# A post-norm block's feed-forward residual: added token by token on GpSimd and VectorE in place of TensorE products with the identity, and the second normalisation in fused steps

## What is computed

```python
x1 = layernorm(r1) * ln1_g + ln1_b
ff = maximum(x1 @ W1 + b1, 0) @ W2 + b2        # 128 -> 512 -> 128
y  = layernorm(x1 + ff) * ln2_g + ln2_b
x3 = layernorm(x + y)                           # x: the block's input, no gain
```

## Time and profile before

| | |
|---|---|
| median of 3 runs | 623.52 us (620.82 to 624.37) |
| the profiled execution | 623.5 us |
| its span, first to last instruction | 621.7 us |
| mean granted TensorE clock | 0.97 |
| instructions | 42741 |

### The profile page before, as it was taken

The page is one execution under the profiler, slowest core; times in us unless marked ns, Lnnn a source line. Parts: engine busy times, 40 slices in busy tenths (PEclk is TensorE's granted clock), DMA queues, the critical chain, the costliest instruction groups (busy, mean ns, idle before and its releaser), DMA issues.

```text
span 621.7 us, 42741 instructions
## 1 busy us (share of the span) xinstructions
PE 518.8 (83%) x18003; PEld 442.0 (71%) x18003; DVE 520.0 (84%) x1761; ACT 440.1 (71%) x877; POOL 405.1 (65%) x523
## 2 busy tenths in 40 slices
PE   0269999999999789998565798898889888898886
PEld 0148888888888566777534688787777777787775
DVE  5547898989899377786478799999999999999982
ACT  3336776767777537776327589988898888988892
POOL 8425537555552235364127789988998888988992
PEclk9989999999999899999678799999999999999999
DMA  6875985755545200100001323332333223332232
GB/s 202 263 230 179 275 249 173 207 162 175 160 129 184 92 17 23 30 17 1 9 10 39 75 52 82 84 74 61 80 80 84 68 63 84 80 80 68 68 79 49
DMA packets 45198, 64.33 MB, mean 103 GB/s; under 512 B 5488, under 2 KB 37360, under 8 KB 42608
## 3 DMA queue, kind: packets, MB, share of 16 engines
q1 hardware_dynamic: 45168, 63.97, 37.1%
HBM read 36.29 MB, written 8.65 MB: 72 GB/s over the span
## 4 chain that ended last, share of the span: by engine, by line
PE 37%; DVE 35%; issue 14%; POOL 5%; DMA 3%; SPq 2%; ACT 2%; DVEq 1%; POOLq 0%; ACTq 0%
PE ps L758 7%; DVE top L1409 7%; DVE hid L1458 6%; DVE prod L1467 5%; PE ps L817 5%; DVE r_x L1452 4%; PE ps L738 4%; PE ps L830 4%; PE ps L773 4%; DVE best L1420 4%; PE ps L748 3%; PE ps L784 2%; PE ps L923 2%; DMA prod<-terms 2%; SPq L403 1%
## 5 line engine op out<-in xcount | busy, mean ns | idle before, releaser
L972 ACT ACTIVATE arena<-ps 128x512 f32<-128x512 f32 x128 | 69.8, 595 | 54.9 <-PE ps L758 54.7
L923 PE MATMUL ps<-arena,hid 128*32 128x32 f32 x8192 | 78.8, 199 | 30.8 <-DVE hid L1458 26.6
L923 PEld LDWEIGHTS ps<-arena,hid 128*32 128x32 f32 x8192 | 75.3, 111 | 36.4 <-DVE hid L1458 14.3
L1200 DVE TENSOR_REDUCE row_max<-ps 128x8 f32<-128x768 f32 x64 | 61.0, 953 | 20.7 <-PE ps L748 20.4
L932 PEld LDWEIGHTS ps<-xT,downT_sb 128*128 128x128 f32 x528 | 66.7, 198 | 12.6 <-issue 11.7
L758 PE MATMUL ps<-ident,arena 128*128 128x128 f32 x512 | 69.6, 281 | 0.0
L944 PE MATMUL ps<-up_sb,prod 128*128 128x128 f32 x528 | 67.7, 282 | 0.3 <-DVE prod L1467 0.3
L932 PE MATMUL ps<-xT,downT_sb 128*128 (+1 forms) x528 | 66.6, 281 | 0.0
L738 PE MATMUL ps<-tile_rows 100*32 100x96 bf16 x2112 | 36.7, 214 | 35.7 <-POOL tile_rows L563 24.9
L1203 DVE TENSOR_TENSOR arena<-ps,row_max 128x768 f32<-128x768 f32 x64 | 61.3, 958 | 5.2 <-DVE row_max L1200 2.2
L672 POOL TENSOR_TENSOR wq_sb<-wq_sb,tile_rows 128x1024 f32<-128x1024 f32 x32 | 65.1, 2034 | 0.7 <-POOL tile_rows L666 0.6
(11 more groups left out here) (164 smaller groups left out, 1359.1 us busy)
## 6 DMA issues: line engine op xcount, KB each, us to landing
arena<-r_x SPq DMA_DIRECT2D x128, 128.0 KB, 2.4
early<-terms SPq DMA_DIRECT2D x8, 720.0 KB
xT<-terms SPq DMA_DIRECT2D x8, 720.0 KB
hid<-terms SPq DMA_DIRECT2D x8, 720.0 KB
prod<-terms SPq DMA_DIRECT2D x8, 720.0 KB
x_pair<-in_x_wrapped SPq DMA_DIRECT2D x16, 256.0 KB, 4.1
xT_tile<-xT SPq DMA_DIRECT2D x34, 64.0 KB, 1.9
x<-in_x SPq DMA_DIRECT2D x8, 256.0 KB, 2.8
```

The costliest lines, as they stand in the source:

```text
L923: mm = nc.tensor.matmul(slots[32 * g:32 * g + 32, k, c], leftT[p][:, r // 2, r % 2, :], blocks_of[p][:, :, r // 2, r % 2, GROUP * g:GROUP ...
L972: return nc.scalar.activation(out_ap, in_ap, ACT.Copy)
L1200: V.tensor_reduce(mx.rearrange("p (a b) -> p a b", a=2), sc, AX_X, ALU.max).then_inc(max_done, 1)
```

## The change

The residual no longer goes through TensorE. GpSimd makes `x1_b2` = y1 * ln1_g + (ln1_b + b2) token by token, in two 128x512 instructions (`x1_and_b2`), for batch 0 at the end of the attention stage and for batch n + 1 behind the second root of batch n, ahead of `x_and_bias`. VectorE adds it to the output products in `ln2_stats`, into `r2` in SBUF, and takes the statistics from there. The second normalisation becomes two bursts of four 128x128 scalar_tensor_tensor: `ln2_centre`, (r2 - mean) * ln2_g, in place in r2, ahead of the wait for the roots, and `ln2_apply`, r2 * rstd + x_lnb. ScalarE's second eviction and TensorE's eight identity products go. The gain ln1_g and the sum ln1_b + b2 are now held as 128x128 rows, so there are ten early weights in place of eight, the last pair after SP's pair of tiles 9.

```diff
@@ buffers
-        b2_col = sb("b2_col", [P, 1])
-        out_bias = sb("out_bias", [P, 1])
+        ln1_g_all = sb("ln1_g_all", [P, P])
+        x1_bias_all = sb("x1_bias_all", [P, P])
-        x1T_b2 = tile_rows[:, 512:1024]
+        x1_b2 = tile_rows[:, 512:1024].rearrange("p (a d) -> p a d", a=4)
@@ SP
-        N_WEIGHTS = 8
+        N_WEIGHTS = 10
-                    (ln2_b_all[:], row(ln2_b)), (b2_col[:], col(b2)),
+                    (ln2_b_all[:], row(ln2_b)), (scratch[:], row(b2)),
+                    (ln1_g_all[:], row(ln1_g)), (x1_bias_all[:], row(ln1_b)),
-                    for dst, src in itertools.islice(weights, 0 if i >= 9 else 2):
+                    for dst, src in itertools.islice(weights, 0 if i >= 10 else 2):
@@ GpSimd
+            def x1_and_b2(n, q):
+
+                pool.wait_ge(y1_done, n + 1)
+                need(pool, residual_added, n)
+                hold(pool)
+                nc.gpsimd.tensor_tensor(x1_b2, y1[q], bcast(ln1_g_all[:], 1, 4), ALU.mult).then_inc(x1_step, 1)
+                pool.wait_ge(x1_step, n + 1)
+                hold(pool)
+                nc.gpsimd.tensor_tensor(x1_b2, x1_b2, bcast(x1_bias_all[:], 1, 4), ALU.add).then_inc(x1_b2_ready, 1)
+
             rsqrt(0, 1, 3)
             x_and_bias(0, 0, 0)
             pool.wait_ge(pv_done, GROUPS * NT)
+            pool.wait_ge(bias_summed, 1)
+            x1_and_b2(0, 0)
...
                     rsqrt(2 * n + 2, 0, 1)
                     if not (last and q == 1):
+                        x1_and_b2(n + 1, 1 - q)
                         x_and_bias(n + 1, i + q, 1 - q)
@@ TensorE
             def y1_transpose(n, q):
                 pe.wait_ge(y1_done, n + 1)
-                need(pe, x1T_b2_done, n)
+                need(pe, x1T_copied, n)
...
             def output_products(n, q):
 
-                pe.wait_ge(x1T_b2_done, n + 1)
-                need(pe, r2_normed, n - 1)
-                for a in range(4):
-                    nc.tensor.matmul(ps[:, 3 + 3 * q, a * P:(a + 1) * P], x1T_b2[:, a * P:(a + 1) * P], ident[:],
-                                     start=(a == 0), stop=False, skip_group_check=True)
+                need(pe, residual_added, n - 1)
                 pe.wait_ge(relu_done, FC * (n + 1))
                 for a in range(4):
                     for c in range(FC):
                         mm = nc.tensor.matmul(ps[:, 3 + 3 * q, a * P:(a + 1) * P], hidT[:, c, a * P:(a + 1) * P],
-                                              w2_sb[:, c, :], start=False, stop=(c == FC - 1), skip_group_check=True)
+                                              w2_sb[:, c, :], start=(a == 0 and c == 0), stop=(c == FC - 1),
+                                              skip_group_check=True)
@@ ScalarE
-                nc.scalar.activation(x1T_b2[:], ps[:, 0, :], ACT.Identity, bias=out_bias[:], scale=ln1_g_col[:]
-                                     ).then_inc(x1T_b2_done, 1)
...
-            a.wait_ge(bias_summed, 1)
             hidden(0)
@@ VectorE
             def ln1_apply(n, q, place=1):
                 need(v, x1T_done, n - 1)
+                need(v, x1_b2_ready, n - 1)
                 ln_apply(place, r1[q], y1[q], y1_done)
 
             def ln2_stats(n, q):
                 v.wait_ge(ff2_done, n + 1)
-                return ln_stats(0, ps[:, 3 + 3 * q, :].rearrange("p (a d) -> p a d", a=4))
+                v.wait_ge(x1_b2_ready, n + 1)
+                V.tensor_tensor(r2, ps[:, 3 + 3 * q, :].rearrange("p (a d) -> p a d", a=4), x1_b2, ALU.add
+                                ).then_inc(residual_added, 1)
+                v.wait_ge(residual_added, n + 1)
+                return ln_stats(0, r2)
+
+            def ln2_centre(n, q):
+
+                for a in range(4):
+                    last = V.scalar_tensor_tensor(r2[:, a, :], r2[:, a, :], moments[:, a, 0:1], ln2_g_all[:],
+                                                  ALU.subtract, ALU.mult)
+                last.then_inc(r2_normed, 1)
 
             def ln2_apply(n, q):
-
-                ln_apply(0, ps[:, 3 + 3 * q, :].rearrange("p (a d) -> p a d", a=4), r2, r2_normed)
                 v.wait_ge(r2_normed, n + 1)
-                V.tensor_tensor(r2, r2, bcast(ln2_g_all[:], 1, 4), ALU.mult).then_inc(r2_scaled, 1)
-                v.wait_ge(r2_scaled, n + 1)
                 v.wait_ge(xlnb_ready, n + 1)
                 need(v, x3_done, n)
-                V.tensor_tensor(r3, r2, x_lnb[q][:], ALU.add).then_inc(r3_done, 1)
+
+                for a in range(4):
+                    last = V.scalar_tensor_tensor(r3[:, a, :], r2[:, a, :], rstd[:, a:a + 1], x_lnb[q][:, a, :],
+                                                  ALU.mult, ALU.add)
+                last.then_inc(r3_done, 1)
...
-                    V.tensor_tensor(out_bias[:], ln1_b_col[:], b2_col[:], ALU.add).then_inc(bias_summed, 1)
+                    V.tensor_tensor(x1_bias_all[:], x1_bias_all[:], scratch[:], ALU.add).then_inc(bias_summed, 1)
...
                     ln2_stats(n, q).then_inc(stat_step, 1)
                     ln_moments(2 * n + 2, 0, 1)
+                    ln2_centre(n, q)
                     v.wait_ge(rstd_done, 2 * n + 2)
```

More of the change, by code:

```diff
@@ L269, in attention_and_product_keys @@
         bias_summed = sem("bias_summed")
-        x1T_b2_done = sem("x1T_b2_done")
+        x1_step = sem("x1_step")
+        x1_b2_ready = sem("x1_b2_ready")
+        residual_added = sem("residual_added")
         x1T_done = sem("x1T_done")
@@ L281, in attention_and_product_keys @@
         r2_normed = sem("r2_normed")
-        r2_scaled = sem("r2_scaled")
         r3_done = sem("r3_done")
```

## The result

The changed kernel takes 631.08 us (median of 4 runs, 630.01 to 631.94), the kernel before 622.63 us beside it (620.82 to 624.37): ratio 1.012, 95% interval 1.0094 to 1.0147. It is slower by about 8.5 us; 12.5 were forecast. One execution in all that follows (675.38 us at a mean granted TensorE clock of 0.753, of the kernel with the fused steps alone) was in a slower state of the chip and is left out of its median.

The account below looks back on a forecast made before the run. TensorE was taken to bound the feed-forward before the change, GpSimd's row after it. Through batch 5 +12.2 us, batch 6 +0.35, batch 7 about nothing: +12.5 on 623.5 gave 636.0 us, range 625 to 641.

Parts of the forecast that it names:

- The mechanism: Feed-forward: VectorE's SBUF-to-SBUF steps stand still beside GpSimd's 128x512 instructions; batch 12.4 us in place of 10.25.
- TensorE's gain: Feed-forward batch: without eight identity products, output products wait for the last ReLU; 0.28 us gained, loop 9.97 us.
- VectorE's own costs: VectorE alone, per batch: added addition 0.69 us, each fused burst of four 1.11; round in 8.3 us.
- Root done at +6.3: Steady batch, counted from its start at 260.44: GpSimd's second reciprocal root ends 6.3 us in.
- Three of the seven slip in, four follow: VectorE's seven steps left after the root: three pass during GpSimd's row, four follow it, taking 1.1 us.
- Some 5.0 with three insertions: GpSimd's row behind the second root holds the port 4.76 us, some 5.0 with three VectorE steps inserted.
- Costed at nothing: Attention stage: one more pair of weight loads, 1.3 us once if uncovered; bias sum at most 0.28 once; both taken as 0.
- two steps per boundary: Rival in the feed-forward: two VectorE steps pass per GpSimd boundary, about 631 us; two or three together had chance 0.25.
- No lock: Rival: VectorE's new bursts are not held beside GpSimd, TensorE stays the bound; -2.9 us, about 620.6; chance 0.12.
- shut out: Rival: VectorE's seven steps all wait for the last of GpSimd's row; about 640 us; chance 0.15.
- The signs named beforehand: Feed-forward: batches 12 to 12.7 us apart, TensorE about 80% busy waiting for ln1_apply, held VectorE steps about 1.2 us each.
- one step per boundary: Main case: one VectorE step passes between two GpSimd instructions; batch 12.4 us, total 636; chance 0.45.

Follow-up runs that it names:

- the kernel with the fused steps alone: Kernel before with only the second normalisation as two bursts of four fused steps, residual still through TensorE: median 623.12 us, ratio 0.9983.
- The pair moved: Changed kernel with GpSimd's two new instructions of a batch put behind the zero fill and VectorE's last burst: median 625.33 us, ratio 1.0042 to the kernel before.
- left out: Changed kernel without GpSimd's two new instructions in batches 1 to 7: median 621.35 us, ratio 0.9965 to the kernel before.
- cut up: Changed kernel with each of GpSimd's two new 128x512 instructions cut into four of 128x128, same place: median 622.34 us, ratio 0.9991 to the kernel before.
- The kernel with the loads: Kernel before with later tiles placed as in the changed kernel and two more weights loaded, ten in all: 622.85 us, ratio 0.999.

## Why the prediction was right, and where its size was off

- **The mechanism** was right: VectorE's steps from SBUF behind the second root stand still beside GpSimd's 128x512 instructions, one passes per boundary, and GpSimd's row becomes the pace. The pair moved, left out and cut up each took the cost away.
- **TensorE's gain** of 0.28 us a batch: the batch was 9.88 to 9.97 where VectorE was free. Right.
- **VectorE's own costs**: addition 0.69, burst 1.14 (1.11 taken). Right. By the estimate from the Trainium skill (VectorE: DVE Perf Modes, "The TRN2 errata", about 150 cycles of fixed latency) it would have been 1.16; the trace lies between.
- **Root done at +6.3**: 272.18 + 1.01 = 273.19 is 6.31 behind 266.88. Right.
- **"Three of the seven slip in, four follow"** is the step whose size was off. Where GpSimd waits for its own semaphore, its port is free for 0.18 us and two steps passed, so three steps remain at the fill's end (the held one and two more), not four: 0.28 less. "Some 5.0 with three insertions" allowed 0.24 for VectorE delaying GpSimd; from 273.15 to 278.17 the row is only 0.12 longer than reckoned (most of it the fill, 1.10 in place of 1.03). From root to next batch 5.68 us in place of 6.1, batch 11.9 on average in place of 12.4.
- **By batches**, from the first root to the last third statistics: batch 0 +2.2 (3.1 forecast), batches 1 to 5 +6.5 (9.1), batch 6 -0.8 (+0.35), batch 7 -0.3 (0); sum 7.7 for 12.5. Batch 6 is the same error at its largest: with only four steps to pass, the extra one meant that none was left for the fill, a microsecond (its burst began at 296.40 and was through at 300.03, the fill at 300.92).
- **Costed at nothing**: the pair of loads and the bias sum. The kernel with the loads is at 0.999 of the kernel before. The sum takes 0.29 us, once, at 197.80; no run tries it alone. Right as far as shown.
- **The rivals**: two steps per boundary was true of one of the four boundaries, the one with the gap. Its figure, 631, is what was measured, but by its own working (0.83 us a batch less than 12.4) batches would be 11.6 us, and they are 11.9. The totals agree by luck: batches 1 to 5 came out 1.6 us above its sum, batches 6 and 7 1.4 below. "No lock" and "shut out" fall with the steps' rows above.
- **The signs named beforehand**: batches were to be 12 to 12.7 us apart and TensorE about 80% busy; they are 11.85 to 11.99 and 85%, just outside, by the same missed step. TensorE waits for ln1_apply and the held steps take 1.29 to 1.37 us, as said.
- **A weak premise**: one step per boundary was taken from a cast beside a memset. Those rows do not show it cleanly, as said above. That it came nearly right here rests on the rows of the changed kernel, not on them.

## What to carry to other kernels

Before moving elementwise work to an idle GpSimd, look at what VectorE does at that moment: steps that read two SBUF tensors, or tensor_scalar from SBUF to SBUF, stand still until the GpSimd instruction that reads SBUF is over (1.3 us for a step of 0.3 beside 128x512), while steps from PSUM (1.37 for four) and statistics (0.87 for four) run on. An engine with time to spare is not enough; ask for a place beside steps that don't share the port. If there is none, cut GpSimd's instructions narrow: each boundary lets a waiting step through, and two passed where GpSimd waited 0.18 us for a semaphore.

## What the runs showed of the hardware that was not expected

A GpSimd instruction is delayed too when VectorE's instruction is long: 1.27 became 1.71 and 1.03 became 1.50 beside a 128x512 multiplication and addition that take 0.69 us alone, where narrow steps cost it only 0.02 to 0.09. And cutting GpSimd's 128x512 into four (0.42 to 0.48 a step) made it 40% longer (3.61 us for 2.56) and the batch 1.9 us shorter.
